# The order of a routed step in a mixture-of-experts kernel: gate products, turns, up products, down products of two blocks back

## The reference

```
h = cond_linear(x, cond)                      # base matrix and low-rank part
scores = softmax(h @ gate_w.T)                # 4096 x 8
topk_w, topk_i = top_k(scores, 2)
topk_w = topk_w / (topk_w.sum(-1) + 1e-20) * 2.5
g = silu(h @ w_gate[e]) * (h @ w_up[e])       # 256 -> 352, each expert e
expert_out = g @ w_down[e]                    # 352 -> 256
y = sum of topk_w * expert_out over the two experts of a token
out = x + y + (silu(h @ sw_gate) * (h @ sw_up)) @ sw_down    # shared, 704 wide
```

## Time and profile before

| | |
|---|---|
| three timed runs | 505.87, 511.4 and 512.41 us, median 511.4 |
| profiled execution | 506.99 us, of which the span from the first to the last instruction is 505.3 |
| TensorE, busy | 490.5 us |
| VectorE, busy | 355.4 us |
| ScalarE, busy | 261.1 us |
| GpSimd, busy | 249.9 us |
| routed stage on TensorE | from 185.5 to 432.7 us of the span |

### The profile page before, as it was taken

How to read it: one execution, slowest core, us unless ns; L and a number is a source line. 1 busy time by engine, 2 the same in 40 slices (tenths; PEclk the granted TensorE clock), 3 DMA queues, 4 the chain that set the end, 5 groups by cost and what they waited for, 6 DMA issues and landing times.

```text
span 505.3 us, 10018 instructions
## 1 busy us (share of the span) xinstructions
PE 490.5 (97%) x3071; PEld 448.2 (89%) x3072; DVE 355.4 (70%) x765; ACT 261.1 (52%) x525; POOL 249.9 (49%) x367
## 2 busy tenths in 40 slices
PE   8999999999999999989999999999999899999996
PEld 7998988888888889988889999999998899888886
DVE  3666778898987556766676677676675666479896
ACT  3567785556663445565455555545554444444322
POOL 2042246655551454666967767677667674211100
PEclk9999999999999999999999999999999999999999
DMA  8387569156222234534344444444444442599942
GB/s 225 130 281 224 169 186 310 57 179 201 45 83 43 84 93 126 119 103 125 104 114 116 114 116 123 123 117 117 112 114 116 115 105 68 145 370 322 384 140 83
DMA packets 104938, 74.54 MB, mean 148 GB/s; under 512 B 61946, under 2 KB 99844, under 8 KB 104900
## 3 DMA queue, kind: packets, MB, share of 16 engines
q1 hardware_dynamic: 95780, 55.21, 37.1%
q0 software_dynamic: 6816, 18.62, 12.5%
q10 hardware_dynamic: 2304, 0.26, 0.5%
HBM read 40.25 MB, written 20.32 MB: 120 GB/s over the span
## 4 chain that ended last, share of the span: by engine, by line
PE 75%; DVE 15%; ACT 5%; issue 4%; DMA 1%; another core or an unknown queue 0%; DVEq 0%; ACTq 0%
PE bank L274 17%; PE bank L276 17%; PE bank L275 17%; PE bank L790 9%; PE bank L762 5%; PE bank L792 5%; DVE bank L1222 2%; ACT gt_h L952 1%; DVE acc L1333 1%; DVE xt_l L1034 1%; ACT x_half L872 1%; DVE x L1058 1%; DVE pos L1081 1%; DMA xin<-in_x_dram 1%; PE bank L576 1%
## 5 line engine op out<-in xcount | busy, mean ns | idle before, releaser
L274 PE MATMUL bank<-w_all,rt_h 128*128 x284 | 97.6, 344 | 0.0
L276 PE MATMUL bank<-w_all,rt_l 128*128 x284 | 91.6, 323 | 0.0
L275 PE MATMUL bank<-w_all,rt_h 128*128 x284 | 91.5, 322 | 0.0
L790 PE MATMUL bank<-w_all,gt_h 128*128 (+1 forms) x213 | 78.0, 396 | 0.2 <-issue 0.2
L551 POOL DMA_INDIRECT y_rows<-y_sb,dst_i x71 | 72.5, 1021 | 11.2 <-POOL spare L465 10.4
L544 POOL DMA_INDIRECT rows<-x_halves,tok_i x71 | 69.5, 978 | 12.5 <-issue 2.2
L952 ACT CAST gt_h<-bank 128x512 fp32r<-128x512 f32 (+1 forms) x48 | 28.1, 586 | 88.7 <-DVE bank L1222 79.8
L274 PE MATMUL bank<-xs_h,sg_h 128*128 128x512 f32 x176 | 70.6, 401 | 0.3 <-DVE gt_h L1233 0.3
L275 PE MATMUL bank<-xs_l,sg_h 128*128 128x512 f32 x176 | 68.9, 391 | 0.0
L276 PE MATMUL bank<-xs_h,sg_l 128*128 128x512 f32 x176 | 68.7, 390 | 0.0
L1295 DVE TENSOR_TENSOR g<-bank,act 128x352 f32<-128x352 f32 x71 | 37.2, 524 | 41.7 <-issue 24.5
(11 more groups left out here) (180 smaller groups left out, 1155.6 us busy)
## 6 DMA issues: line engine op xcount, KB each, us to landing
pick<-y_rows SPq DMA_DIRECT2D x16, 512.0 KB, 7.8
xin<-in_x_dram SPq DMA_DIRECT2D x8, 512.0 KB, 4.8
x_halves<-x_half SPq DMA_DIRECT2D x8, 512.0 KB, 3.3
w_own<-in_L_ffn_w_gate_dram SPq DMA_DIRECT2D x8, 352.0 KB, 4.5
w_own<-in_L_ffn_w_up_dram SPq DMA_DIRECT2D x8, 352.0 KB, 4.7
y_sb<-in_x_dram SPq DMA_DIRECT2D x5, 512.0 KB, 3.5
base_rows<-y_sb SPq DMA_DIRECT2D x5, 512.0 KB, 2.8
acc<-base_rows SPq DMA_DIRECT2D x5, 512.0 KB, 7.1
```

What stands on the lines that cost most here:

```text
L274: pe.matmul(o, lh, rh, start=start, stop=False, skip_group_check=skip)
L275: pe.matmul(o, lh, rl, start=False, stop=False, skip_group_check=skip)
L276: return pe.matmul(o, ll, rh, start=False, stop=stop, skip_group_check=skip)
L790: pe.matmul(YE[par][:, 0:2 * D].rearrange("p (h d) -> p h d", h=2), gt_h[par][0:n, cols], both, start=(c == 0), stop=False, skip_group_che ...
```

## The change

TensorE's step for block i becomes: gate products of block i, turns of g of block i-1, up products of block i, down products of block i-2. The loop is gone; all 71 steps are written out, and the register with the expert of block i+1 is loaded between the gate products and the turns. The gate products wait for the silu of block i-1, since bank 0 is written again. At the start, the gate and up products of block 0 go ahead of the down products of shared units 28 and 29; at the end, the down products of blocks 69 and 70 lie within the first two shared units. ScalarE rounds g's high part behind the silu of the next block instead of ahead of it. VectorE multiplies block i-1 first, then writes words and low part of block i+1, then adds up y of block i-3, then writes g's low part. GpSimd makes six gathers ahead instead of five.

```diff
-            for i in range(5):
+            for i in range(6):
                 gather(i)
             for i in range(NBLK):
-                if i + 5 < NBLK:
-                    gather(i + 5)
+                if i + 6 < NBLK:
+                    gather(i + 6)
...
+            def e_gate(i, e):
+                pe.wait_ge(s_rtl, i + 1)
+
+                pe.wait_ge(s_act, UE + i if i >= 1 else UE - 1)
+                e_into(EG, i, e, 0, s_G)
+
+            def e_up(i, e):
+                if i == 0:
+                    pe.wait_ge(s_gl, UE - 1)
+                e_into(EU, i, e, F, s_U)
...
+            experts = [expert_of(0)]
+            for i in range(NBLK):
+                e_gate(i, experts[i])
+                if i + 1 < NBLK:
+                    experts.append(expert_of(i + 1))
+                if i >= 1:
+                    e_turn_g(i - 1)
+                e_up(i, experts[i])
+                if i == 0:
+                    down(*order[NPRE - 2])
+                    down(*order[NPRE - 1])
+                elif i >= 2:
+                    e_down(i - 2, experts[i - 2])
+
+
             for v, (j, c) in enumerate(order[NPRE:]):
                 gate(j, c)
                 if v >= 2:
                     down(*order[NPRE + v - 2])
                 if v == 0:
-                    e_down(NBLK - 1, (NBLK - 1) % 2, before)
+                    e_turn_g(NBLK - 1)
+                if v < 2:
+                    e_down(NBLK - 2 + v, experts[NBLK - 2 + v])
                 up(j, c)
...
                 if i + 1 < NBLK:
                     r_word_high(i + 1)
-                e_high(i - 1)
-                if i + 1 < NBLK:
                     r_high(i + 1)
...
                 e_silu(i)
+                e_high(i - 1)
...
-            e_mul(0)
-            base(NPG - 1)
             for i in range(1, NBLK):
+                e_mul(i - 1)
                 if i + 1 < NBLK:
                     r_word_low(i + 1)
-                if i >= 2:
-                    e_y(i - 2)
+                    r_low(i + 1)
+                if i == 1:
+                    base(NPG - 1)
+                if i >= 3:
+                    e_y(i - 3)
                 e_low(i - 1)
-                if i + 1 < NBLK:
-                    r_low(i + 1)
-                e_mul(i)
+            e_mul(NBLK - 1)
+            e_y(NBLK - 3)
+            e_low(NBLK - 1)
             e_y(NBLK - 2)
...
                 mul(j, c)
+                if n == 0:
+                    e_y(NBLK - 1)
```

More of the change, by code:

```diff
@@ L52, in adaln_moe @@
     UP = NPRE + NBLK
-    TURN = 12
     WARM = 14
@@ L248, in adaln_moe @@
         EG, EU, TB, YE = bank[0], bank[1], bank[2], bank[6:8]
-        def known(i, below):
-            return isinstance(i, int) and i < below
         def unit(j, c):
@@ L683, in gate @@
                     pe.wait_ge(s_x1, NT)
-                elif u < NPRE or u > UP + 1:
+                elif u == UP:
+                    pe.wait_ge(s_act, UP)
+                elif u == UP + 1:
+                    pe.wait_ge(s_gl, UP)
+                else:
                     if c == 1:
@@ L745, in _ @@
                     rank()
-            down(*order[NPRE - 2])
             pe.wait_ge(s_wlo, N_PART * E)
@@ L753, in expert_of, with e_into @@
                 _, es = nc.values_load_multi_w_load_instructions(
-                    blk_e[0:1, bass.ds(b, 1)], engines=[mybir.EngineType.PE], min_val=0, max_val=E - 1,
+                    blk_e[0:1, b:b + 1], engines=[mybir.EngineType.PE], min_val=0, max_val=E - 1,
                     skip_runtime_bounds_check_because="VectorE clips them to E - 1", bass_reorder=False)
                 return es[0]
+            def e_into(to, i, e, c, ready):
+                par = i % 2
+                for k in range(K):
+                    wh, wl = (w_all[:, h, bass.ds(e, 1), k * 2 * F + c:k * 2 * F + c + F]
+                              .rearrange("p e f -> p (e f)") for h in range(2))
+                    mm = three_pass(pe, to[:, 0:F], rt_h[par][:, k * P:(k + 1) * P], rt_l[par][:, k * P:(k + 1) * P],
+                                    wh, wl, k == 0, k == K - 1)
+                mm.then_inc(ready, 1)
+            def e_gate(i, e):
[6 more added lines that the diff above has]
+                e_into(EU, i, e, F, s_U)
             def e_turn_g(i):
-                pe.wait_ge(s_g, i + (UE + 1))
+                pe.wait_ge(s_g, UE + i + 1)
                 for c in range(FC):
@@ L763, in e_turn_g, with e_down @@
                 mm.then_inc(s_gT_e, 1)
[L765 to L782, removed]
+            def e_down(i, e):
+                par = i % 2
+                pe.wait_ge(s_gl, UE + i + 1)
+                if i >= 2:
                     pe.wait_ge(s_y, i - 1)
@@ L1311, in _ @@
             r_low(1)
-            e_mul(0)
-            base(NPG - 1)
             for i in range(1, NBLK):
+                e_mul(i - 1)
                 if i + 1 < NBLK:
                     r_word_low(i + 1)
-                if i >= 2:
-                    e_y(i - 2)
+                    r_low(i + 1)
[3 more added lines that the diff above has]
+                    e_y(i - 3)
                 e_low(i - 1)
-                if i + 1 < NBLK:
-                    r_low(i + 1)
-                e_mul(i)
+            e_mul(NBLK - 1)
+            e_y(NBLK - 3)
+            e_low(NBLK - 1)
             e_y(NBLK - 2)
-            e_low(NBLK - 1)
-            e_y(NBLK - 1)
             def mix(j, to, picks, counted, before, some_of):
```

## The result

The changed kernel takes 521.39 us (median of four runs, 518.72 to 525.78), the kernel before beside it 508.63: a ratio of 1.026, with a 95% interval from 1.014 to 1.038. It is slower (the interval lies above 1), and outside the range that was given. The profiled execution took 519.43 us with a span of 517.7.

The account below looks back on a forecast made before the run. TensorE, busy 97% of the span, was taken as the bound. On the profiled 506.99 us, -9.7 stalls, +8.4 chain, +0.5 entry and +2.4 exit gave 508.6; with 1.5 carried from timed runs, 510 us, range 501.5 to 518.

Parts of the forecast that it names:

- Order of a step: TensorE's routed steps: six gate products, 0.96 us, more cover for VectorE's multiplication; gain 8.6 to 9.7 us of stalls.
- Loop and register load: Routed stage: back edges already counted in the 9.7 us; moved expert load hidden by queued products, taken as 0.
- late signal: Routed stage: remaining late signals cost only where TensorE would wait for the gathering chain anyway; nothing added.
- the chain: Words, y, scatter, gather, transposing, words: closes over three blocks, a step not under 3.42 us; 8.4 us lost.
- a short idle ahead of nearly every turn or gate product: Expected sign in TensorE's profile after the change if the forecast is right, with steps some 3.4 us apart.
- the time from gather to words: Transfer part of the gathering chain, taken as 6.33 us; its changing with the new order was named the main risk.
- longer steps leave the transfers more room: Argument against the hard-chain rival, in which late transfers feed themselves and steps take 3.65 us.
- The sixth gather "only keeps the distance": GpSimd's extra early gather keeps the distance between gather and scatter, since y comes a step later; no gain counted.
- Entry: Start of routed stage: TensorE stands 1.0 us before block 0's gate products, 0.50 idle before turns goes; net +0.5.
- Exit: End of routed stage: picked rows come 2.7 us later, 2.4 returning as a TensorE stall; VectorE's wait about 5.
- The sum: Whole kernel: -9.7 + 8.4 + 0.5 + 2.4 = +1.6 us against the profiled execution of 506.99, that is 508.6.
- the chain binds hard: Rival, chance 0.10: gathering chain with 7.01 us from gather to words, 3.65 a step, kernel at 526 us.

Follow-up runs that it names:

- e14: Kernel before with six early gathers instead of five, each held until the down products of six blocks back have ended: 505.96 us, ratio 0.993.
- e12: Changed kernel with seven early gathers, each held until the up products of four blocks back have ended: 503.13 us, ratio 0.989 to the kernel before.
- e4: Kernel before with only its loop on the chip written out: 508.10 us, ratio 1.000.
- e9: Changed kernel with seven early gathers and fixed expert numbers, so no register loads: 513.40 us, ratio 1.009 to the kernel before.
- e2: Changed kernel with seven gathers ahead of the scatters instead of six, nothing else: 511.86 us, ratio 1.010 to the kernel before.
- e3: Changed kernel with five early gathers instead of six, nothing else: 623.68 us, one run.
- e15: Changed kernel with seven gathers held as in e12, and entry and exit as in the kernel before: 502.79 us, ratio 0.987 to the kernel before.
- e11: Changed kernel with seven early gathers and the turns of block i-1 back ahead of block i's gate products: 517.64 us, ratio 1.014 to the kernel before.

## Why the prediction was wrong, by its own steps

**Order of a step: right in kind, too large.** Six more products of cover were to cure all but 1.1 of 9.7 us of stalls. With the gathers held the stage is 234.2, that is 230.4 + 3.8: of the 9.7 us, 5.9 went, and what is left is a handful of steps: behind the entry, behind GpSimd's own work of 2.5 us (below), and around block 59. The hold is in that figure too; the kernel before with held gathers has a stage of 239.1 (e14), 8.1 us of stalls. As times, e14 (0.993) and e12 (0.989) can not be told apart.

**Loop and register load: right.** Both were put at nothing; e4 and e9 show nothing. The price of the Trainium skill for loading a register (Runtime: NRT & Kernel Launch, section on instruction fetch mechanics), an estimated 14 us if exposed, is not seen here: without the loads the ratio is 1.009 instead of 1.010.

**What failed: the stalls that the new order keeps, put at nothing.** The sum took the whole 9.7 us as gone, and said of the rest: "What a late signal still costs falls where TensorE would wait for this chain anyway; I add nothing for it." The changed kernel has 20.1 us of stalls, and they do not hide behind the chain. In e2 the chain is open, and ScalarE waits for rows only twice; even so its profiled execution, 4 us above its median, has a stage of 246.3, with 15.9 us of stalls. With the hold, 3.8 are left. In per cent of the kernel before: the new order with held gathers is at -1.1 (e12), letting seven gathers follow y adds 2.1 (e2), the sixth in place of the seventh, which closes the chain over three steps, adds 1.6; that makes the 2.6 that were measured. Each part is uncertain by about 1. In time the last two are some 11 and some 8 us. The prediction had the 8, and not the 11.

**The chain: there, and of about the size that was given.** "Three steps can then not be shorter than 1.46 + 2.47 + 6.33 = 10.26" gave 8.4 us, and the seventh gather is worth some 8. The form was wrong. The prediction expected "a short idle ahead of nearly every turn or gate product"; most steps are undisturbed, and the stalls are few and long. In the turn shown above GpSimd waits for y and the last words for the transfer, so that a late transfer can make the next y and the next gather late; the prediction named this for its rival only. The time from gather to words, of which it said "I would be wrong above all if" it changed, hardly did: 6.52 in the mean, where it took 6.33, and 6.83 between the same starts in the kernel before. So nothing here speaks against "longer steps leave the transfers more room". One slip changes nothing: with 6.44 the chain gives 11.0, not 10.8.

**The sixth gather "only keeps the distance": right**, as e3 shows by its absence.

**Entry: right in size** (0.99 us of idle ahead of the first gate products, 1.0 predicted, and the 0.50 ahead of the first turns is gone). **Exit: mis-sized.** The wait for the picked rows grew from 2.2 to 2.4, not to 5, and TensorE's stall is 0.85, not 2.4. In e15, which has both ends as before, neither is to be seen in the time. Why the picked rows came as early as before was not followed up.

**The sum.** -9.7 + 20.1 in the stage and 2.0 outside it make the 12.4 us between the profiled spans; predicted were -9.7 + 8.4 and 2.9. In number the result is near the rival that was given 0.10, "the chain binds hard" (3.65 a step and 526 us; measured 250.5 / 70 = 3.58 and 521.4), and the range was cut below it. That nearness is luck: the rival rested on 7.01 us from gather to words, and these took 6.52.

**Still open** is how a gather that follows y stalls TensorE when the rows come in good time. The count of late blocks does not answer it. In 31 of the 44 of the changed kernel VectorE went to the multiplication straight from the instruction before, as here in block 31 (last up product, low part of g of the block before, multiplication):

```profile
298.97 0.32 PE L271 MATMUL bank<-w_all,rt_l 128*128 x1
...
300.03 0.55 DVE L1297 TENSOR_TENSOR gt_l<-bank,gt_h 128x384 fp32r<-128x384 f32 x1
...
300.49 0.52 DVE L1293 TENSOR_TENSOR g<-bank,act 128x352 f32<-128x352 f32 x1
```

There it is VectorE's own list that is behind, not a signal of TensorE; only in the other 13 did VectorE stand before it. Nor does the count go with the time: e11 has 5 and is slow, e15 has 16 and the lowest median. Which transfer or engine begins a stall was not found.

## What to carry to other kernels

In a ring of engines where loads are issued behind stores, ask what releases the next load. If it is a result that the load itself delays, the ring sets a pace of its own; counting the steps over which it closes tells where that begins (one step less cost 102 us, one more gave some 8). But opening the ring was not enough: the cure was to release the load by the engine that sets the pace, by a wait whose cost no measurement shows. And a change that is slower as a whole can hide a gain: with the gathers held it is 1.1% under the kernel before. How much of that is the order is not shown, since the old order with held gathers is 0.7% under it.

## What the hardware showed that was not expected

**A stall of TensorE can be paid twice.** The view of stretches of the changed kernel (us, busy time and count of TensorE, its weight loads, VectorE, ScalarE, GpSimd, then the granted clock) behind the step of 5.85 us:

```profile
248.00:249.00 1.00, 1.00 (x8) 0.85 (x6) 0.80 (x1) 0.90 (x3) 0.98 (x2) 1.00 0.72 149
249.00:250.00 1.00, 0.26 (x2) 0.00 (x0) 1.00 (x1) 0.48 (x1) 1.00 (x2) 1.00 0.30 98
250.00:251.00 1.00, 0.00 (x0) 0.00 (x0) 1.00 (x2) 0.00 (x0) 0.71 (x1) 1.00 0.00 0
251.00:252.00 1.00, 0.86 (x5) 0.86 (x6) 1.00 (x4) 0.00 (x0) 0.18 (x1) 1.00 0.58 131
252.00:253.00 1.00, 0.81 (x7) 0.53 (x6) 0.72 (x3) 0.24 (x1) 0.98 (x1) 0.98 0.00 0
253.00:254.00 1.00, 1.00 (x5) 1.00 (x5) 0.81 (x2) 0.90 (x3) 0.83 (x3) 0.50 0.34 139
254.00:255.00 1.00, 1.00 (x4) 1.00 (x4) 0.72 (x3) 0.04 (x1) 0.82 (x3) 0.50 0.00 0
```

TensorE was busy for 0.26 us of the microsecond from 249, not at all in the next, and for 0.86 of the third; at 253 the granted clock is 0.50, the lower of its two levels, and four or five products fit in a microsecond instead of eight. That falls into the next step, of 4.91 us.

**That stall came behind a VectorE instruction that took long beside GpSimd.** In the timeline of the changed kernel:

```profile
248.19 2.51 POOL L499 TENSOR_TENSOR xs_l<-xs_w,xs_h 128x512 fp32r<-128x512 f32 x2
248.21 2.80 DVE L1262 TENSOR_TENSOR rt_l<-rt_w,rt_h 128x256 fp32r<-128x256 f32 x1 [0.67 <-ACT rt_h L963]
```

The low part of the rows takes 0.43 us elsewhere; here it took 2.80, beside two GpSimd instructions of 2.51 together. The Trainium skill (SBUF — State Buffer, section "Who interferes with whom") says that VectorE and GpSimd share a pair of ports that one of them locks for a whole instruction. The rows agree, and here VectorE was held over two; no run takes the GpSimd work away to prove it. The same pair of instructions stands in the kernel before, where the low part took 1.68 us, and in e12, where it took 2.95; there the step took 4.27 us, and the granted clock stayed at 1.00.
